# Four conditioned residual layers on one core: TensorE's register load of the language number is moved from behind layer 3's matmuls to the head of each pass

## The chip, the cores and the metric

The kernel runs on one core of a Trainium2 chip. The metric is the device time of one execution in microseconds (us). The kernel before took a median of 1185.27 us in 3 runs (1184.71 to 1189.29).

## The reference, cut to what matters

There are 128 samples, each a 128 x 512 matrix in fp32. Each sample passes through four residual layers, and each layer picks its weights by a number that belongs to the sample. The third number, the language, is the one that the change concerns.

```python
x = x + (einsum('bnh,boh->bno', x, W0[subject]) + b0[subject])          # L0
x = x + rotate_pairs(x, amplitudes ** delta_t, frequencies * delta_t)    # L1
x = x + (einsum('bsd,bdh->bsh', x, W2[category]) + b2[category])         # L2
h = relu(einsum('bsh,bha->bsa', x, W1[language]) + b1[language])         # L3
y = x + einsum('bsa,bah->bsh', h, Wup[language]) + bup[language]
x = x + layernorm(y) * gamma[language] + beta[language]
```

## The kernel before, in words

The samples are sorted by subject, so that the 1 MB matrix of layer L0 is fetched only when the subject changes (8 times). `ids` is a small SBUF tile with the sorted numbers. Each engine that needs a number reads it there into a register with `value_load`, which the trace shows as three instructions of the engine's sequencer: TENSOR_LOAD, FUSED_REGOPS and SEQ_ASSERT. Line 228 is the load of the language number (`language_of`) on whichever engine calls it, line 231 that of the "first of its subject" flag, line 222 that of the subject, line 219 that of the sample's number.

Each engine has an instruction order written out by hand, a software pipeline over the samples. Semaphores tie the engines together. TensorE (PE) does, in pass s of its loop:

- `l0_front(s + 1)`: the first 6 of L0's 12 matmuls for the next sample (lines 879 and 883). It first waits for x1 and for the rounded x, at line 877.
- `l2(s)`: L2's 12 matmuls, 4 each at lines 918, 922 and 928. The four at line 928 read `w2_lo`, the low part of the weights, which VectorE (DVE) makes in two halves at line 741. The first and the third of the four wait for one half each.
- `language_of(pe, s - 1)`: the register load.
- `l0_back(s + 1)`: the other 6 matmuls of L0 (lines 890 and 896).
- `transpose_x3(s)`: four transposes (line 938).
- `up(s - 1, lang_before)`: three matmuls with the up-projection of the sample before (lines 958, 959, 961). Their weights' address comes from the register, so this is the first place that needs the number.
- `rotate(s + 1)`: L1 as 8 short matmuls (line 907).
- `down(s)`: 8 short matmuls (line 948) on the transposed x3, which ScalarE (ACT) copies out of PSUM in four parts at line 578. Each pair of matmuls waits for its part.

The order around the loads on other engines: ACT reads the language number (line 228) once a pass, after it has copied the rotated sample (line 540), and GpSimd (POOL) reads the flag of line 231 at about the same time. SyncE (SP) issues the DMAs in this order in each step: the next L2 weights (line 289, 1 MB), the bias row (line 297, after a wait for the x3 that DVE makes at line 763), the store of a finished sample (line 312), the next x (line 281), then the flag's load (line 231), the subject's (222) and the ordinal's (234), and L3's weights (line 306). SP's steps run in a hardware loop of 12 steps a round.

Of the kernel before, what the change touches and what calls it, by code (L numbers as in the profile page):

```python
# [18 lines left out]
def conditioned_residual_stack(  # L19
# [32 lines left out]
    with ctx:  # L52
# [174 lines left out]
        def language_of(eng, s):  # L227
            return eng.value_load(ids[0:1, bass.ds(3 * B + s, 1)], min_val=0, max_val=L - 1)
# [612 lines left out]
        def _(pe):  # L841
# [26 lines left out]
            def l0_front(s):  # L868

                if s == 0:  # L870
                    pe.wait_ge(w0_hi_made[0], 1)
                    pe.wait_ge(w0_hi_made[1], 1)
                if s == 1:
                    pe.wait_ge(diag_made, 2)
                if s >= 1:
                    pe.wait_ge(x1_made, s)
                pe.wait_ge(x_hi_made, s + 1)
                for c in range(C):
                    pe.matmul(ps_l0[:, :], x_hi[s % 2][:, c * N:(c + 1) * N], w0_hi[:, c * D:(c + 1) * D],  # L879
                              start=(c == 0), stop=False)  # L880
                pe.wait_ge(x_lo_made, s + 1)
                for c in range(C // 2):
                    pe.matmul(ps_l0[:, :], x_lo[s % 2][:, c * N:(c + 1) * N], w0_hi[:, c * D:(c + 1) * D],  # L883
                              start=False, stop=False)

            def l0_back(s):


                for c in range(C // 2, C):
                    pe.matmul(ps_l0[:, :], x_lo[s % 2][:, c * N:(c + 1) * N], w0_hi[:, c * D:(c + 1) * D],  # L890
                              start=False, stop=False)
                if s == 0:
                    pe.wait_ge(b0_made, 2)
                    pe.wait_ge(w0_lo_made, 4)
                for c in range(C):
                    mm = pe.matmul(ps_l0[:, :], x_hi[s % 2][:, c * N:(c + 1) * N], w0_lo[:, c * D:(c + 1) * D],  # L896
                                   start=False, stop=(c == C - 1))
                mm.then_inc(l0_done, 1)

            def rotate(s):  # L900

                if s >= 1:
                    pe.wait_ge(x2T_lo_made, s)
                pe.wait_ge(mix_made, s + 1)
                pe.wait_ge(x1_made, s + 1)
                for c in range(C):
                    mm = pe.matmul(ps_mix[:, c * N:(c + 1) * N], x1[:, c * P:(c + 1) * P], mix[:, :],  # L907
                                   start=True, stop=True)
                mm.then_inc(mix_done, 1)

            def l2(s):

                if s >= 1:
                    pe.wait_ge(x3_made, s)
                pe.wait_ge(w2_hi_made, 2 * s + 2)
                pe.wait_ge(x2T_hi_made, s + 1)
                for c in range(C):
                    pe.matmul(ps_l2[:, :], x2T_hi[:, c * N:(c + 1) * N], w2_hi[:, c * D:(c + 1) * D],  # L918
                              start=(c == 0), stop=False)
                pe.wait_ge(x2T_lo_made, s + 1)  # L920
                for c in range(C):
                    mm = pe.matmul(ps_l2[:, :], x2T_lo[:, c * N:(c + 1) * N], w2_hi[:, c * D:(c + 1) * D],  # L922
                                   start=False, stop=False)
                mm.then_inc(l2_hi_done, 1)
                for c in range(C):
                    if c in (0, C // 2):
                        pe.wait_ge(w2_lo_made, 2 * s + 1 + c // (C // 2))
                    mm = pe.matmul(ps_l2[:, :], x2T_hi[:, c * N:(c + 1) * N], w2_lo[:, c * D:(c + 1) * D],  # L928
                                   start=False, stop=(c == C - 1))
                mm.then_inc(l2_done, 1)  # L930

            def transpose_x3(s):

                if s >= 1:
                    pe.wait_ge(x3T_made, C * s)
                pe.wait_ge(x3_made, s + 1)
                for c in range(C):
                    mm = pe.transpose(ps_x3T[:, c * N:(c + 1) * N], x3[s % X3B][:, c * P:(c + 1) * P], ident[:, :])  # L938
                mm.then_inc(x3T_done, 1)

            def down(s):

                pe.wait_ge(w1_loaded[s % 2], landed(s, 2))
                if s >= 1:
                    pe.wait_ge(h_made, s)
                for c in range(C):
                    pe.wait_ge(x3T_made, C * s + c + 1)
                    mm = pe.matmul(ps_hT[:, :], w1_in[s % 2][:, c * A:(c + 1) * A], x3T[:, c * N:(c + 1) * N],  # L948
                                   start=(c == 0), stop=(c == C - 1))
                mm.then_inc(hT_done, 1)  # L950

            def up(s, lang):

                y, here = ps_y[s % 2], bass.ds(lang * D, D)
                if s >= 2:
                    pe.wait_ge(out_made, s - 1)
                pe.wait_ge(h_hi_made, s + 1)
                pe.matmul(y[:, :], h_hi[:, :], wup_hi[:, here], start=True, stop=False)
                pe.matmul(y[:, :], h_hi[:, :], wup_lo[:, here], start=False, stop=False)
                pe.wait_ge(h_lo_made, s + 1)  # L960
                pe.matmul(y[:, :], h_lo[:, :], wup_hi[:, here], start=False, stop=True).then_inc(up_done, 1)  # L961
# [7 lines left out]
            pe.wait_ge(ids_made, 2)  # L969

            for s in range(B):
                if s < LAST:
                    l0_front(s + 1)
                l2(s)
                lang_before = language_of(pe, s - 1) if s >= 1 else None
                if s < LAST:
                    l0_back(s + 1)
                transpose_x3(s)
                if s == 1:
                    pe.wait_ge(wup_hi_made, len(wup_parts))  # L980
                    pe.wait_ge(wup_lo_made, len(wup_parts))
                if s >= 1:
                    up(s - 1, lang_before)
                if s < LAST:
                    rotate(s + 1)
                down(s)
# [51 lines left out]
```

## Time and profile before

| | |
|---|---|
| median of 3 runs | 1185.27 us |
| the profiled execution's own time | 1189.29 us |
| its span, first to last instruction | 1187.5 us |
| mean granted TensorE clock | 0.977 of full speed |
| PE busy (matmul) | 1124.6 us, 95% |
| DVE, ACT, POOL busy | 913.6, 797.2, 772.2 us |
| chain that ended last | PE 49%, SP's queue 28%, issue 13%, DMA 5% |

Durations below come from the profiled execution, whose own time lies 4.0 us above the median of the runs. An engine's name with a q (PEldq, SPq) means its sequencer: loads of registers, waits and the issue of DMAs, which don't count as busy. PEld is the weight load of a matmul, PE the matmul. Matmuls of 512 columns follow each other every 0.23 us in full flow, though the profile gives each a duration of 0.39 us, because they overlap.

### The profile page before, as it was taken

How to read it: one execution, taken by the hardware profiler on the slowest of the kernel's cores; microseconds unless marked ns; L12 is line 12 of the kernel's file. 1: busy time of each engine (PE TensorE's matmuls, PEld its weight loads, DVE VectorE, ACT ScalarE, POOL GpSimd, SP SyncE). 2: the span in 40 equal slices, each digit the busy share in tenths (PEclk: the TensorE clock that was granted, in tenths of full speed). 3: DMA queues.
4: the chain of work that ended last, by engine and by line, in shares of the span. 5: the costliest groups of instructions: out<-in, count | busy, mean ns of one | idle time of the engine just before them, and what ended most of it. 6: DMA issues, size and time to landing. Idle time of an engine off the chain costs nothing.

```text
span 1187.5 us, 29696 instructions
## 1 busy us (share of the span) xinstructions
PE 1124.6 (95%) x6040; PEld 932.9 (79%) x6040; DVE 913.6 (77%) x1345; ACT 797.2 (67%) x1828; POOL 772.2 (65%) x793
## 2 busy tenths in 40 slices
PE   5879999999999998999998999999999999999996
PEld 2768878887888877888887788878887888788884
DVE  5758788787777886777777778788787777778786
ACT  3647777777676766667766667677666766667674
POOL 6256676666666676666666666667676667666664
PEclk9889999999999999899999899999998999999998
DMA  7787886777677688767767776787688678867772
GB/s 255 266 301 234 259 271 221 241 262 268 221 257 238 225 259 262 250 219 242 249 222 264 245 256 215 245 286 244 220 254 282 215 248 251 270 217 253 243 256 78
DMA packets 96847, 289.90 MB, mean 244 GB/s; under 512 B 11406, under 2 KB 12046, under 8 KB 78828
## 3 DMA queue, kind: packets, MB, share of 16 engines
q1 hardware_dynamic: 95756, 287.22, 73.9%
q14 instruction: 175, 1.43, 0.4%
q8 instruction: 52, 0.85, 0.3%
q10 hardware_dynamic: 864, 0.40, 0.1%
HBM read 253.74 MB, written 33.84 MB: 242 GB/s over the span
## 4 chain that ended last, share of the span: by engine, by line
PE 49%; SPq 28%; issue 13%; DMA 5%; DVE 2%; POOL 1%; ACT 1%; ACTq 0%; DVEq 0%; POOLq 0%
SPq L219 6%; PE ps_hT L948 6%; PE ps_l L879 6%; PE ps_l L928 5%; PE ps_mix L907 5%; PE ps_l L918 5%; PE ps_l L922 5%; PE ps_l L896 5%; SPq L231 4%; PE ps_l L890 3%; PE ps_l L883 3%; DMA b_in<-b 3%; PE ps_x3T L938 2%; SPq L222 2%; SPq L234 2%
## 5 line engine op out<-in xcount | busy, mean ns | idle before, releaser
L741 DVE TENSOR_TENSOR w_lo<-w_in,w_hi 128x1024 fp32r<-128x1024 f32 x256 | 310.4, 1254 | 0.0
L446 POOL TENSOR_TENSOR x<-x,beta_sb 128x512 f32<-128x512 f32 x128 | 173.5, 1355 | 159.7 <-DVE ps_y L776 143.7
L533 ACT ACTIVATE w_hi<-w_in 128x1024 fp32r<-128x1024 f32 x256 | 255.3, 1045 | 8.5 <-PE ps_l L922 8.4
L578 ACT ACTIVATE x3T<-ps_x3T,minus_bup 128x128 f32<-128x128 f32 x512 | 146.5, 368 | 87.9 <-PE ps_x3T L938 87.8
L416 POOL TENSOR_TENSOR w_in<-w_in,ident 128x512 f32<-128x512 f32 x128 | 165.1, 1290 | 50.4 <-DMA w_in<-W 49.8
L756 DVE TENSOR_TENSOR x2T_lo<-ps_mix,x2T_hi 128x512 fp32r<-128x512 f32 x128 | 88.5, 691 | 116.1 <-ACT x2T_hi L540 116.1
L422 POOL TENSOR_TENSOR x_lo<-x_in,x_hi 128x512 fp32r<-128x512 f32 x128 | 166.1, 1298 | 7.0 <-ACT x_hi L505 4.7
L879 PE MATMUL ps_l<-w_hi,x_hi 128*128 128x512 f32 x512 | 156.2, 428 | 2.2 <-issue 2.2
L433 POOL TENSOR_TENSOR rstd<-var_eps,minus_half 128x1 f32<-128x1 f32 x128 | 141.4, 1104 | 18.9 <-POOL var_eps L428 0.2
L948 PE MATMUL ps_hT<-x3T,w_in 128*128 128x128 f32 x1024 | 141.5, 283 | 11.5 <-ACT x3T L578 11.5
L907 PEld LDWEIGHTS ps_mix<-mix,x 128*128 128x128 f32 x1024 | 125.5, 193 | 34.0 <-issue 34.0
L907 PE MATMUL ps_mix<-mix,x 128*128 128x128 f32 x1024 | 143.0, 283 | 5.2 <-DVE x L749 5.1
L428 POOL TENSOR_SCALAR var_eps<-square_sum 128x1 f32<-128x1 f32 x128 | 55.4, 433 | 141.7 <-ACT squares L565 140.6
L928 PE MATMUL ps_l<-w_lo,x2T_hi 128*128 128x512 f32 x512 | 139.3, 392 | 2.3 <-DVE w_lo L741 2.2
L948 PEld LDWEIGHTS ps_hT<-x3T,w_in 128*128 128x128 f32 x1024 | 129.8, 199 | 13.1 <-issue 13.1
L918 PE MATMUL ps_l<-w_hi,x2T_hi 128*128 128x512 f32 x512 | 139.6, 395 | 0.0
L896 PE MATMUL ps_l<-w_lo,x_hi 128*128 128x512 f32 x512 | 138.7, 393 | 0.0
L922 PE MATMUL ps_l<-w_hi,x2T_lo 128*128 128x512 f32 x512 | 136.9, 389 | 0.0
L763 DVE TENSOR_TENSOR x<-ps_l,b_in 128x512 f32<-128x512 f32 x128 | 88.5, 692 | 56.3 <-PE ps_l L928 56.3
L498 ACT ACTIVATE ps_diag<-ident,cos 128x128 f32<-128x128 f32 x128 | 47.6, 372 | 121.9 <-DVE mix L718 121.8
L776 DVE SCALAR_TENSOR_TENSOR ps_y<-ps_y,x 128x512 f32<-128x512 f32 x128 | 89.5, 699 | 45.4 <-PE ps_y L961 45.4
L918 PEld LDWEIGHTS ps_l<-w_hi,x2T_hi 128*128 128x128 f32 x512 | 98.1, 192 | 22.0
(108 smaller groups left out, 1914.2 us busy)
## 6 DMA issues: line engine op xcount, KB each, us to landing
w_in<-W SPq DMA_DIRECT2D x128, 1024.0 KB, 5.9
x_in<-xT SPq DMA_DIRECT2D x128, 256.0 KB, 4.5
w_in<-W SPq DMA_DIRECT2D x128, 256.0 KB, 2.6
b_in<-bias_rows SPq DMA_DIRECT2D x128, 256.0 KB, 5.5
out<-yb SPq DMA_DIRECT2D x128, 256.0 KB, 5.0
w_in<-W0T SPq DMA_DIRECT2D x8, 1024.0 KB, 4.8
wup_sb<-Wup SPq DMA_DIRECT2D x1, 2560.0 KB, 9.5
gamma_sb<-gamma SPq DMA_DIRECT2D x1, 2560.0 KB, 9.3
```

Source lines behind the costliest of these rows:

```text
L416: pool.tensor_tensor(diagonal_of(w2_in[s % WB]), diagonal_of(w2_in[s % WB]), ident[:, :].unsqueeze(1).broadcast_to([P, C, P]), ALU.add).th ...
L422: pool.tensor_tensor(x_lo[s % 2][:, :], x_in[s % XB][:, :], x_hi[s % 2][:, :].bitcast(fp32), ALU.subtract).then_inc(x_lo_made, 1)
L446: pool.tensor_tensor(x3[s % X3B][:, :], x3[s % X3B][:, :], beta_sb[:, bass.ds(lang * D, D)], ALU.add)\
L533: act.activation(w2_hi[:, halves[n]], w2_in[s % WB][:, halves[n]], ACT.Copy).then_inc(w2_hi_made, 1)
L741: dve.tensor_tensor(w2_lo[:, half], w2_in[s % WB][:, half], w2_hi[:, half].bitcast(fp32), ALU.subtract).then_inc(w2_lo_made, 1)
L879: pe.matmul(ps_l0[:, :], x_hi[s % 2][:, c * N:(c + 1) * N], w0_hi[:, c * D:(c + 1) * D], start=(c == 0), stop=False)
L896: mm = pe.matmul(ps_l0[:, :], x_hi[s % 2][:, c * N:(c + 1) * N], w0_lo[:, c * D:(c + 1) * D], start=False, stop=(c == C - 1))
L907: mm = pe.matmul(ps_mix[:, c * N:(c + 1) * N], x1[:, c * P:(c + 1) * P], mix[:, :], start=True, stop=True)
L918: pe.matmul(ps_l2[:, :], x2T_hi[:, c * N:(c + 1) * N], w2_hi[:, c * D:(c + 1) * D], start=(c == 0), stop=False)
L922: mm = pe.matmul(ps_l2[:, :], x2T_lo[:, c * N:(c + 1) * N], w2_hi[:, c * D:(c + 1) * D], start=False, stop=False)
L928: mm = pe.matmul(ps_l2[:, :], x2T_hi[:, c * N:(c + 1) * N], w2_lo[:, c * D:(c + 1) * D], start=False, stop=(c == C - 1))
L948: mm = pe.matmul(ps_hT[:, :], w1_in[s % 2][:, c * A:(c + 1) * A], x3T[:, c * N:(c + 1) * N], start=(c == 0), stop=(c == C - 1))
```

## The change: the load of the language number comes first in the pass

In pass s, TensorE now reads the language number of sample s - 1 ahead of `l0_front(s + 1)`, which is right behind `down(s - 1)` of the pass before, and no longer between `l2(s)` and `l0_back(s + 1)`. The number of instructions is the same, and so is the register's use in `up(s - 1)`. The last load, for `up(LAST)` behind the loop, stays.

```diff
             for s in range(B):
+                lang_before = language_of(pe, s - 1) if s >= 1 else None
                 if s < LAST:
                     l0_front(s + 1)
                 l2(s)
-                lang_before = language_of(pe, s - 1) if s >= 1 else None
                 if s < LAST:
                     l0_back(s + 1)
                 transpose_x3(s)
```

## Rows read from the trace of the kernel before

**Rows 1.** Busy us in 668:728: PE, PEld, DVE, ACT, POOL; clock, DMA share, GB/s.
```profile
668.00:728.00 60.00, 60.00 (x340) 51.16 (x339) 47.14 (x72) 42.59 (x100) 41.41 (x43) 1.00 0.72 231
```
**Rows 2.** Waits over the whole span: total us, times, longest.
```profile
PEld ps_l L890 <- issue: 13.3, 39, 0.6
...
PE ps_hT L948 <- ACT x3T L578: 11.5, 7, 1.8
...
SPq L297 <- DVE x L763: 9.7, 13, 1.6
```
**Rows 3.** Timeline, one pass (start us, us, what, number of instructions).
```profile
497.40 2.35 DVE L741 TENSOR_TENSOR w_lo<-w_in,w_hi 128x1024 fp32r<-128x1024 f32 x2
...
500.83 0.62 PE L890 MATMUL ps_l<-w_hi,x_lo 128*128 128x512 f32 x2
...
502.99 1.14 ACT L578 ACTIVATE x3T<-ps_x3T,minus_bup 128x128 f32<-128x128 f32 x4 [0.64 <-PE ps_x3T L938]
...
503.27 0.97 PEld L907 LDWEIGHTS ps_mix<-mix,x 128*128 128x128 f32 x8 [0.21 <-issue]
503.33 1.09 PE L907 MATMUL ps_mix<-mix,x 128*128 128x128 f32 x8
...
505.08 1.17 PE L879 MATMUL ps_l<-w_hi,x_hi 128*128 128x512 f32 x4
```
**Rows 4.** Line 228 from 499 to 510: duration ns min/median/max, first and last start.
```profile
L228 PEldq TENSOR_LOAD <-ids x2: 297/299/301, 499.8 to 508.2; - x2
...
L228 PEldq SEQ_ASSERT  x2: 18/18/18, 500.4 to 508.8; - x2
```
**Rows 5.** Line 877, the wait ahead of l0_front, from 503.9 to 505.6.
```profile
L877 PEldq EVENT_SEMAPHORE  x1: 51/51/51, 504.2 to 504.2; - x1
```
**Rows 6.** The last load (line 228, from 1175.5) and ACT's copies before it.
```profile
L228 PEldq TENSOR_LOAD <-ids x1: 303/303/303, 1176.5 to 1176.5; - x1
...
1175.34 1.15 ACT L578 ACTIVATE x3T<-ps_x3T,minus_bup 128x128 f32<-128x128 f32 x4 [3.71 <-PE ps_x3T L938]
```
**Rows 7.** Register loads over the whole span, by line and engine.
```profile
L228 PEldq TENSOR_LOAD <-ids x128: 295/307/1051, 46.6 to 1176.5; - x128
...
L231 SPq TENSOR_LOAD <-ids x127: 263/512/1063, 34.7 to 1147.2; - x127
```
**Rows 8.** The chain from 510 to 519, and the load of that pass (line 228).
```profile
516.95 0.91 PE ps_l L928 x4
517.85 0.10 issue
517.96 0.72 PE ps_l L890 x2
...
L228 PEldq TENSOR_LOAD <-ids x1: 942/942/942, 516.7 to 516.7; - x1
```
**Rows 9.** ACT's load of line 228 in 95:156, 487:506, 668:721 and 924:935.
```profile
L228 ACTq TENSOR_LOAD <-ids x7: 506/967/1112, 97.2 to 147.8; - x7
...
L228 ACTq TENSOR_LOAD <-ids x3: 592/928/1072, 487.7 to 504.5; - x3
...
L228 ACTq TENSOR_LOAD <-ids x7: 583/749/1110, 668.6 to 719.2; - x7
...
L228 ACTq TENSOR_LOAD <-ids x2: 714/718/721, 925.2 to 933.7; - x2
```
**Rows 10.** SP's issue of the store, timeline from 494 to 505.
```profile
503.18 0.36 SPq L312 DMA_DIRECT2D out<-yb  x1
```
**Rows 11.** Two single loads of PE with the store issued before each.
```profile
953.42 0.36 SPq L312 DMA_DIRECT2D out<-yb  x1
...
L228 PEldq TENSOR_LOAD <-ids x1: 944/944/944, 954.3 to 954.3; - x1
...
887.98 0.36 SPq L312 DMA_DIRECT2D out<-yb  x1
...
L228 PEldq TENSOR_LOAD <-ids x1: 298/298/298, 888.8 to 888.8; - x1
```

## The prediction

> **What bounds the kernel now.** I read the page first: PE is busy for 1124.6 us of 1187.5, and no other engine passes 914. The table of busy time by stretch then shows that in the middle of the kernel PE has no hole at all, 60.00 us of 60.00, at full granted clock [rows 1]. So any delay of a matmul there is a delay of the end. The page's chain says that this isn't so everywhere: 49% of it lies on PE, but 28% on SP's sequencer, which feeds the DMAs; in SP's stretches some us of PE are free. The list of waits comes next. The weight load of line 890, the first instruction behind the old place of the register load, was held up 39 times, 13.3 us together, by nothing but issue [rows 2]. That is the register load's present price, seen at the weight load.
>
> The timeline of one pass with the register loads beside it gives the mechanism. DVE ends the second half of w_lo at 497.40 + 2.35 = 499.75 [rows 3], and PE's load starts at 499.8 [rows 4]. The last load of the kernel shows the same at the other place: ACT's copies end at 1175.34 + 1.15 = 1176.49, and the load starts at 1176.5, while `down`'s matmuls, which the copies feed, are still running [rows 6]. So the sequencer hands matmuls on ahead of time, but a register load starts only when the last semaphore wait ahead of it is met, here 0.05 us later. What is ahead of it in the queue then covers it, or doesn't.
>
> A rule of the Trainium skill bears on this. "TensorE: Matmul & The Clock Gate", in its table and its section on the array, gives TensorE a queue of 64 instructions. By it alone one would expect the load to run far ahead of the matmuls at either place and to cost nothing. The trace agrees only in part: a few matmuls are queued, but the start is tied to the semaphore [rows 3, 4].
>
> **The change part by part.** The edit moves one load per pass, 127 in all. Nothing is added, and no DMA or semaphore moves.
>
> *Taken away at the old place.* The weight load normally runs one matmul (0.23 us) ahead of its matmul, and 0.06 us is the least (503.27 to 503.33 [rows 3]), so each of the 39 gaps hides some 0.17 us: 13.3 - 39 x 0.17 = 6.7 us reach the matmuls. The pass at 517 checks it: the load took 0.942, and the chain has 0.10 of issue and 0.72 for two matmuls that otherwise take 0.45, so 0.37 us were lost [rows 8]. Part of the 6.7 lies in stretches that SP sets. With 49% of the chain on PE I take 3.5 us as the gain, with bounds 0 and 6.7.
>
> *Cost at the new place, ordinary load.* The last wait ahead is now the fourth part of ACT's copy in `down(s - 1)`. It ends at 502.99 + 1.14 = 504.13 [rows 3]; the wait of line 877 fires at 504.2 behind it [rows 5]; the load would start at 504.18. The matmul of line 879 starts at 505.08, so there are 0.90 us of room. Needed are the load, 0.29 from its end to the end of SEQ_ASSERT (500.1 to 500.4 [rows 4]), 0.05 for the next step, 0.05 for the wait of line 877 [rows 5], 0.03 for the step behind it, and 0.06 from weight load to matmul: t + 0.48. The limit is t = 0.42 us. The median load takes 0.307 [rows 7], so the ordinary pass loses nothing and has 0.11 us to spare. At the old place the same sum is 500.83 - 499.80 = 1.03 of room for t + 0.29 + 0.05 + 0.06, so the limit was 0.63. The new place is tighter by 0.2 us. Its cover is the eight short matmuls of `down`; if it is lost, each 0.1 us costs 12.7 us.
>
> *Cost at the new place, slow load.* Loads take up to 1.05 us on PE and 1.06 on SP [rows 7]. What decides is the time since SP issued the store of a finished sample (line 312). SP's load of line 231 comes 1.7 us behind that store in every step, and its median is 0.512, twice its minimum [rows 7]. PE's load begun 0.85 us behind a store took 0.944 [rows 11]. So the store opens a slow period, which begins about 0.8 us after it and is over about 2 us after it.
>
> Where does the new load fall? In the passes in which SP has caught up with PE, it waits for x3 (line 763) before the bias row [rows 2] and stores at a fixed place in PE's pass: at 503.18 [rows 10], 1.0 us before the new load's 504.18. The nearest witness is ACT's load of line 228, 0.33 us later than the new one. In these passes it is slow every time: 7 with a median of 0.967, 3 with 0.928, 7 with 0.749, 2 with 0.718 [rows 9]. The old place of PE's load was free of this in those passes. If the slow period is already running at 504.18, the new load ends together with ACT's, so it takes t(ACT) + 0.33, and PE loses t(ACT) + 0.33 - 0.42, and 0.06 more for the second matmul (at the old place the sum gives 0.942 - 0.63 = 0.31, and 0.37 were measured [rows 8]): t(ACT) - 0.03. Sum: 7 x 0.94 + 3 x 0.90 + 7 x 0.72 + 2 x 0.69 = 15.7 us over 19 passes. All lie in stretches where SP waits for PE, so they count in full. If the period hasn't begun, they cost nothing: the bounds are 0 and 15.7. The two single loads at this distance, 0.83 to 0.87 us behind the store, went one each way (0.944 and 0.298 [rows 11]); but in the 19 passes ACT's load was never spared, and most of the new loads fall nearer 1.1 us behind the store. I take four fifths, 12.6 us.
>
> *Passes where a subject changes.* ACT's copies come late there and hold PE's `down` 7 times, 11.5 us [rows 2]. The load then starts late too, with only a pair or two of matmuls as cover, and some 0.5 us come on top each time, unless DVE or POOL are later still. Bounds 0 and 3.5; I take 1.
>
> Sum: -3.5 + 12.6 + 1 = +10.1 us. Against the profiled execution's own 1189.3 that is 1199.4; that execution lies 4.0 above the median of the runs, so the forecast is 1185.3 + 10.1 = 1195.4, taken as 1195.5.
>
> **The rivals.** Half a percent is 5.9 us, about what a measurement of this kernel can tell from no change.
>
> *Hidden after all (no change).* The slow period begins between 1.1 and 1.3 us behind the store, so the new load is back before it. For it speaks the fast load at 0.87 us [rows 11]; against it the slow one at 0.85. The sum is then -3.5 + 0 + 1 = -2.5: 1182.8, with bounds 1179 and 1189.
>
> *The gain alone (faster).* The place behind the matmuls of L2 was the one that met slow loads: in the stretch around 517 the load took 0.942 and cost 0.37 [rows 8]. If the new load misses every slow period and the queue ahead of it is enough even where subjects change, all 6.7 us return: 1178.6. It decides for this side if fewer than 2 passes stall and over 5.9 us of the gain is on the path; much of it lies in stretches set by SP, which speaks against. The queue of 64 in the Trainium skill's "TensorE: Matmul & The Clock Gate" would lead to this side too.
>
> *The ordinary load isn't covered (much slower).* If the sequencer needs 0.1 to 0.2 us more than my 0.48, for instance because the wait of line 877 costs more behind a load, every pass loses 0 to 0.1 us: up to 12.7 us on top, 1208, and to 1215 if slower passes also keep SP caught up with PE for longer, so that more passes stall. The last load of the kernel, 0.303 long, speaks for short loads there [rows 6]. "DMA: Bandwidth & Descriptors", under latency and other measured facts in the Trainium skill, gives a register load a floor of about 600 ns; by it an estimate would add (0.60 - 0.42) x 127 = 23 us. The trace disagrees, with a median of 0.307 [rows 7].
>
> **How the numbers follow.** The forecast's case, stalls in the caught-up passes, has 0.60; hidden after all 0.24; the gain alone 0.07; the ordinary load not covered 0.09. With all 19 passes and 3.5 where subjects change the first case reaches 1185.3 + 15.7 = 1201 and, if the gain isn't on the path, 1204.5; with half of the passes it gives 1190.7. Alone its range is 1190 to 1205. The range of 8 in 10 takes in the hidden case's middle: 1182 to 1206. Faster by over 0.5%: 0.07. Slower by over 0.5%: 0.60 without a low end of 0.06, and 0.09, so 0.63. Within: 0.24 and 0.06, 0.30.
>
> **What would show it.** PE's loads of line 228 start 0.05 us behind the end of ACT's copies; right. The issue waits at line 890 vanish, and new ones stand at line 879, few and long, up to 1 us. They fall into the passes behind a subject change in which SP waits for x3, and there PE's load lasts as long as ACT's plus 0.3 us. A median load of PE far from 0.30 us, small gaps at line 879 in every pass, or fast loads 1.0 us behind the store would prove steps wrong. If SP stands elsewhere in PE's pass, since its own steps slow down or it needs longer to catch up, the number of stalled passes is another one, and the sum with it.

## The result and the profile after

| kernel | runs | median us (lowest to highest) | ratio to the kernel before, 95% interval | span us | clock |
|---|---|---|---|---|---|
| before | 20 | 1184.78 (1180.97 to 1189.29) | 1 | 1187.5 | 0.977 |
| changed | 20 | 1191.71 (1184.87 to 1198.49) | 1.0057 [1.0044, 1.0070] | 1195.5 | 0.971 |

The change costs 6.9 us by the medians. The profiled execution, whose own time is 1197.32, has a span 8.0 us longer. A later series of the same kernel (E5 below) gave 1.0038 [1.0019, 1.0057]; it is slower in both, by about half a percent.

First the page's chain of the changed kernel. PE has 41% of it where it had 49%, and SP's queue 34% where it had 28%.

```profile
PE 41%; SPq 34%; issue 15%; DMA 5%; DVE 2%; POOL 1%; ACT 1%; ACTq 0%; DVEq 0%; POOLq 0%
```

The waits of the changed kernel over the whole span (total us, times, longest) answer to [rows 2]. The issue wait at line 890 is gone. Line 879, the first instruction behind the new place, has one 24 times. ACT still holds `down` 7 times.

```profile
PE ps_hT L948 <- ACT x3T L578: 10.9, 7, 1.8
PEld ps_l L879 <- issue: 10.7, 24, 1.7
...
PE ps_l L879 <- issue: 5.8, 14, 1.4
```

An ordinary pass of the changed kernel, timeline and then the rows of line 228 (ns min/median/max, first and last start), answers to [rows 3, 4].

```profile
560.53 1.14 ACT L578 ACTIVATE x3T<-ps_x3T,minus_bup 128x128 f32<-128x128 f32 x4 [0.63 <-PE ps_x3T L938]
...
561.80 1.06 PE L948 MATMUL ps_hT<-x3T,w_in 128*128 128x128 f32 x8
...
562.62 0.71 PE L879 MATMUL ps_l<-w_hi,x_hi 128*128 128x512 f32 x2
```
```profile
L228 PEldq TENSOR_LOAD <-ids x1: 299/299/299, 561.7 to 561.7; - x1
L228 PEldq FUSED_REGOPS  x1: 151/151/151, 562.1 to 562.1; - x1
L228 PEldq SEQ_ASSERT  x1: 18/18/18, 562.3 to 562.3; - x1
```

ACT's copies end at 560.53 + 1.14 = 561.67, the load starts at 561.7, and line 879's matmul comes at 562.62, 0.95 us behind the copies. That is what it was before (504.13 to 505.08 [rows 3]). The ordinary load is free.

A stalled pass of the changed kernel: the timeline, the load's rows, and the chain from 103.90 on.

```profile
105.22 1.14 ACT L578 ACTIVATE x3T<-ps_x3T,minus_bup 128x128 f32<-128x128 f32 x4 [0.77 <-PE ps_x3T L938]
...
105.34 0.36 SPq L312 DMA_DIRECT2D out<-yb  x1
...
107.96 1.16 PE L879 MATMUL ps_l<-w_hi,x_hi 128*128 128x512 f32 x4 [0.41 <-issue]
```
```profile
L228 PEldq TENSOR_LOAD <-ids x1: 1100/1100/1100, 106.4 to 106.4; - x1
L228 ACTq TENSOR_LOAD <-ids x1: 777/777/777, 106.8 to 106.8; - x1
```
```profile
106.66 0.89 PE ps_hT L948 x8
107.55 0.41 issue
107.96 1.16 PE ps_l L879 x4
```

The load starts 1.07 us behind the store and takes 1.10 us. Line 879 comes 1.60 us behind the copies' end at 106.36, so 0.65 us are lost. The chain shows 0.41 of it as issue. The rest is in the longer spacing of the last matmuls of `down`, which the profile charges to them. The sum of the prediction, t + 0.48 - 0.90, gives 0.68 here. ACT's load began 0.37 us later and was 0.32 shorter: the two ended together.

The load of line 228 in the changed kernel's caught-up stretches, PE and then ACT in each (around 97 to 152, 493 to 512, 673 to 727, 807 to 835 and 933 to 944), answers to [rows 9].

```profile
L228 PEldq TENSOR_LOAD <-ids x7: 537/932/1134, 97.3 to 150.9; - x7
L228 ACTq TENSOR_LOAD <-ids x7: 280/574/875, 97.7 to 151.3; - x7
...
L228 PEldq TENSOR_LOAD <-ids x3: 601/713/1078, 493.3 to 511.0; - x3
L228 ACTq TENSOR_LOAD <-ids x3: 290/551/721, 493.6 to 511.4; - x3
...
L228 PEldq TENSOR_LOAD <-ids x7: 376/683/907, 673.9 to 726.4; - x7
L228 ACTq TENSOR_LOAD <-ids x7: 304/447/557, 674.3 to 726.8; - x7
...
L228 PEldq TENSOR_LOAD <-ids x4: 731/853/1047, 807.2 to 833.9; - x4
...
L228 PEldq TENSOR_LOAD <-ids x2: 720/748/777, 933.4 to 942.1; - x2
```

Such rows time the passes as well. From the first to the seventh of ACT's loads six passes took 50.6 us before (97.2 to 147.8 [rows 9]) and take 53.6 now (97.7 to 151.3); in the third stretch 50.6 became 52.5, in the second, two passes, 16.8 became 17.7 (17.73 before rounding). The stretch around 807 is new: in the trace of before SP stored at another place of the pass (in the first four 0.2 to 0.4 us behind ACT's last copy, and not 1.0 ahead of it), and none of ACT's loads in it was slow.

**Where the time went.** For this table I took the end of ACT's last copy (line 578) in each pass from the traces and summed the differences by kind of stretch. "Caught up": SP waits for PE in them in the changed kernel; passes, counted from 1, 5 to 13, 15 to 17, 50 to 53, 70 to 77, 85 to 89 and 99 to 101. "SP late": the long stretches between two changes of subject (17 to 28, 30 to 41, 53 to 65, 77 to 83, 89 to 97, 101 to 111, 113 to 126). The rest are the start and the passes around a change of subject. An undisturbed pass takes 8.43 us.

```
us                          before   changed    E3      E4     undisturbed
26 passes caught up         219.3    228.8    219.3   219.3    219.3
71 passes, SP late          606.3    599.0    601.8   601.8    598.8
28 passes, the rest         293.0    299.1    296.7   306.7
pass 1 to pass 126         1118.6   1126.9   1117.8  1127.7
```

The changed kernel loses 9.5 us where SP has caught up. It gains 7.4 where SP is late, down to the undisturbed length. Of these, 5.9 are at line 890: from the last matmul of line 928 to the first of line 890, and from that to the second, the starts now stand as close as elsewhere. It loses 6.1 in the rest. The sum is 8.3.

The spacing of PE's matmuls, summed in the same way, tells what the rest is made of: 1.5 us more ahead of line 879, behind the load; 1.3 in the six matmuls of `l0_front`, where the clock is low in two more passes than before; 3.4 at line 928, where PE waits for `w_lo`; and 1.4 less at line 890.

### The profile page after: what moved, and what is told of

Its sections match the earlier page's. It is cut to its first block, busy times and chain, and to the rows that moved or that the text cites. A ratio compares the mean times of both kernels' runs of the same rounds, so it can differ in the third digit from the quotient of the medians.

```text
span 1195.5 us, 29696 instructions
## 1 busy us (share of the span) xinstructions
PE 1127.0 (94%) x6040; PEld 941.5 (79%) x6040; DVE 916.2 (77%) x1345; ACT 799.7 (67%) x1828; POOL 771.7 (65%) x793
## 4 chain that ended last, share of the span: by engine, by line
PE 41%; SPq 34%; issue 15%; DMA 5%; DVE 2%; POOL 1%; ACT 1%; ACTq 0%; DVEq 0%; POOLq 0%
SPq L219 7%; PE ps_l L879 5%; PE ps_hT L948 5%; SPq L231 5%; PE ps_l L918 4%; PE ps_l L928 4%; PE ps_l L922 4%; PE ps_mix L907 4%; PE ps_l L896 4%; SPq L222 3%; SPq L234 3%; DMA b_in<-b 3%; SPq L225 2%; SPq L228 2%; PE ps_l L883 2%
## 5 line engine op out<-in xcount | busy, mean ns | idle before, releaser
L433 POOL TENSOR_TENSOR rstd<-var_eps,minus_half 128x1 f32<-128x1 f32 x128 | 147.5, 1153 | 18.9 <-POOL var_eps L428 0.2
L907 PEld LDWEIGHTS ps_mix<-mix,x 128*128 128x128 f32 x1024 | 126.6, 194 | 34.3 <-issue 34.3
L428 POOL TENSOR_SCALAR var_eps<-square_sum 128x1 f32<-128x1 f32 x128 | 46.8, 366 | 138.2 <-ACT squares L565 137.0
L928 PEld LDWEIGHTS ps_l<-w_lo,x2T_hi 128*128 128x128 f32 x512 | 95.0, 188 | 28.6 <-DVE w_lo L741 9.7
```

## The experiments

Each ratio is to the kernel before, run on the same chip in the same series. Its median was 1193.10 us beside E1 to E4, 1191.81 beside E5 to E8, and 1193.26 beside E9 and E10.

| | kernel | median us | ratio, 95% interval | span us |
|---|---|---|---|---|
| E1 | changed, store last in SP's step | 1164.64 | 0.9774 [0.9749, 0.9799] | 1162.3 |
| E2 | before, store last | 1160.33 | 0.9731 [0.9707, 0.9756] | 1158.5 |
| E3 | load behind l0_front | 1191.24 | 0.9988 [0.9973, 1.0003] | 1186.3 |
| E4 | one load ahead of the loop | 1194.75 | 1.0020 [1.0004, 1.0037] | 1197.0 |
| E5 | changed, again | 1195.86 | 1.0038 [1.0019, 1.0057] | 1197.3 |
| E6 | load behind l0_front, store last | 1156.97 | 0.9703 [0.9680, 0.9726] | 1156.6 |
| E7 | changed, two loads a pass | 1265.43 | 1.0630 [1.0596, 1.0664] | 1261.8 |
| E8 | before, two loads a pass | 1216.41 | 1.0209 [1.0180, 1.0239] | 1211.2 |
| E9 | before, SP reads ahead of its store | 1173.50 | 0.9848 [0.9829, 0.9868] | 1168.4 |
| E10 | changed, SP reads ahead of its store | 1174.59 | 0.9856 [0.9837, 0.9874] | 1171.8 |

### E1 and E2: what opens the slow period

SP's store goes to the end of its step, behind the issue of L3's weights; E1 has PE's load at the new place, E2 at the old.

```diff
                     load_b2(s + 2, k + 2, j + 2)
-                if k >= 2:
-                    store_out(s - 2, j - 2)
                 if k < LAST - 3:
                     load_x(s + 4, k + 4, j + 4)
                     load_w0(s + 4)
                 if k < LAST - 1:
                     load_w1(s + 2, k + 2, j + 2)
+                if k >= 2:
+                    store_out(s - 2, j - 2)
```

> The changed kernel with one thing more: SP issues the store of the finished sample (store_out) as the last DMA of its step, behind L3's weights, and no longer between the bias row and the next x. Theory A (the store opens the slow period for register loads, 0.8 to 2.2 us behind its issue): where SP has caught up with PE the store now comes about 4 us behind PE's load, so PE's loads there take about 0.30 us and the issue waits at line 879 outside the passes where a subject changes vanish; the time falls by 6 to 10 us from the changed kernel, to 1182 to 1186 us. The slow loads turn up 0.8 to 2.2 us behind the store's new place, on whichever engine loads there. Theory B (the fetch of x, line 281, or the stream of L2's weights makes loads slow, not the store): x is now issued where the store was, so PE's loads in the caught-up passes stay slow (0.6 to 1.1 us) and the time stays at 1190 to 1193.

> The kernel before with the store last in SP's step, the control for the run above. Theory A: slow loads move to 0.8 to 2.2 us behind the store's new place here too. PE's load at its old place is hit in other passes than before; its limit is 0.63 us. 1180 to 1188 us, about the same as the kernel before. If the reorder alone were worth several us whatever the load's place, both store-last kernels would gain the same over their own kernels; by theory A the changed kernel gains 6 us or more from it and the kernel before 0 to 4.

The stalls went as the store's theory has it: at line 879 issue waits fell from 24 to 10, and in each caught-up stretch the mean pass is at most 8.46 us. The place of the slow loads settles it. I sorted every register load of all engines (some 1930) by the time since the last issue of a store. Seven slow loads of each run come ahead of the first store and are left out, and so are two of the kernel before at 2.5 to 2.7 us and one of 0.405 us in E1 at 3.5:

```
register loads over 0.4 us, of all, by us behind the store's issue
             0-0.5   0.5-1    1-1.5    1.5-2    2-2.5
before        0      11/38    58/74   114/158   14/140
E1            0      18/73    34/46     6/147     0
E2            0      34/87    29/35     6/129     0
```

The slow loads moved with the store, not with x's, the weights' or the bias row's issue, which now stand elsewhere to it. But the times missed the expectations by far. E1 is 28.5 us and E2 32.8 us below the kernel before of their series, and neither theory had that. Slow loads fell from 206 to 66 and 76. SP's own row shows it (line 231; before 263/512/1063 [rows 7]):

```profile
L231 SPq TENSOR_LOAD <-ids x127: 262/269/290, 34.3 to 1114.4; - x127
```

That is E2. Its chain has 70% on PE and 13% on SP's queue. E9 takes this up.

With the store last the new place still costs 4.3 us more than the old, and the traces say where: passes 68 to 70, 97 to 99 and 111 to 113, each a change of subject, took 21.2, 21.6 and 21.6 us in E1 against 19.4, 20.0 and 20.0 in E2. One of them, first the timeline of E1 and of E2, then their tables of busy time (start:end, length, busy PE, PEld, DVE, ACT, POOL, then clock), E1 and E2 again:

```profile
640.91 2.05 PE L879 MATMUL ps_l<-w_hi,x_hi 128*128 128x512 f32 x4 [0.30 <-issue]
642.75 1.05 PE L883 MATMUL ps_l<-w_hi,x_lo 128*128 128x512 f32 x2
```
```profile
640.98 1.17 PE L948 MATMUL ps_hT<-x3T,w_in 128*128 128x128 f32 x8 [1.76 <-ACT x3T L578]
641.91 1.17 PE L879 MATMUL ps_l<-w_hi,x_hi 128*128 128x512 f32 x4
```
```profile
637.00:640.00 3.00, 1.24 (x12) 1.08 (x11) 2.65 (x4) 3.00 (x8) 3.00 (x2) 1.00 0.71 214
640.91:642.75 1.84, 1.84 (x4) 1.46 (x5) 1.84 (x3) 1.74 (x6) 0.54 (x1) 0.50 0.91 362
```
```profile
638.00:641.00 3.00, 1.22 (x10) 1.02 (x9) 2.54 (x4) 2.94 (x6) 3.00 (x3) 1.00 0.82 226
641.91:643.75 1.84, 1.84 (x10) 1.53 (x10) 1.84 (x3) 1.51 (x6) 0.00 (x0) 1.00 0.97 400
```

In both kernels PE was busy for 1.2 of the 3 us shown first, since `down` waited for ACT's late copies (1.76 us in E2). In E2 PE runs on into line 879 at the granted clock 1.00. In E1 the load, an ordinary one of 0.305 us, leaves a hole of 0.30, and the clock is 0.50, the lower of the two levels (1.2 in place of 2.4 GHz); the four matmuls of line 879 take 2.05 us in place of 1.17. The hole costs 0.3 us, the clock some 1.3.

The hole alone doesn't bring the clock down. E1 has seven such passes, each with a wait of 1.76 us and then a hole of 0.26 to 0.36; the clock fell in three of them, the ones named above, and stayed at 1.00 in the other four. One of these:

```profile
297.28 1.16 PE L879 MATMUL ps_l<-w_hi,x_hi 128*128 128x512 f32 x4 [0.36 <-issue]
```

In E2, with no hole, it stayed at 1.00 in all seven. Nor is the hole needed: in the kernel before the clock was down to 0.50 before line 879, with no hole there, behind four of its six waits of 1.76 us, and in E6 behind one of seven. What else decides isn't shown.

### E3 and E4: is it the cover, and where does the gain go?

E3 puts the load behind `l0_front(s + 1)`, so that the same semaphore starts it but six matmuls of 512 columns stand ahead of it as well. E4 reads once ahead of the loop. It leaves out the other 127 loads, and so most of its up-projections are those of another language; it was meant as a floor for the time.

```diff
             for s in range(B):
-                lang_before = language_of(pe, s - 1) if s >= 1 else None
                 if s < LAST:
                     l0_front(s + 1)
+                lang_before = language_of(pe, s - 1) if s >= 1 else None
                 l2(s)
```
```diff
+            lang_before = language_of(pe, 0)
             for s in range(B):
-                lang_before = language_of(pe, s - 1) if s >= 1 else None
                 if s < LAST:
                     l0_front(s + 1)
```

> The register load stands between l0_front(s + 1) and l2(s). Theory A (a load starts when the last wait ahead of it is met, and what is queued ahead covers it): the last wait ahead is still the fourth part of ACT's copy, or the wait of line 877 behind it, so the load starts within 0.15 us of the same moment as in the changed kernel, but eight short matmuls and six long ones (0.90 + 1.37 us) are ahead. The limit rises to about 1.7 us, above the longest load seen (1.1). Loads in the caught-up passes are as slow as in the changed kernel, and none of them costs anything: no issue waits at line 918, time 1181 to 1184 us. Rival (PE's queue holds only some eight instructions ahead of a register load, or the load waits for the matmuls ahead): the load starts later, behind part of l0_front, and stalls of 0.3 to 0.6 us appear at line 918 in every pass: 1200 us or more.

> PE reads the language number once, ahead of its loop, and uses that of the first sample in every up() of the loop but the last: the other 127 register loads are left out, and so the up-projections of most samples are those of another language. It is the floor for every place of the load. Theory A: as fast as the load between l0_front and l2, 1181 to 1184 us, since SP's pace and the subject changes then set what the loads don't; the 6.7 us that reach the matmuls in the kernel before come back only in part. Rival (all of PE's load time in the trace counts): 1184.8 - 7.7 = 1177 us or less.

E3 still meets slow loads, and they cost nothing. In its first caught-up stretch (line 228):

```profile
L228 PEldq TENSOR_LOAD <-ids x7: 297/835/1144, 95.3 to 145.9; - x7
```

Seven loads with a median of 0.835 us, and the stretch runs at 8.43 a pass. No issue wait is left at lines 890 or 918. Cover is what decides at the new place. Yet E3 is no faster than the kernel before (0.9988, within its interval of 1), and E4, with no load in the loop at all, is not either (1.0020). I had expected 1 to 4 us of gain for both: E3 has 1.9 by the medians, within its interval of nothing, and E4 is 1.7 us slower. Both have the caught-up stretches undisturbed and gain 4.5 us where SP is late, and give 3.7 and 13.7 back in the rest. E3's chain has 38% on SP's queue and 34% on PE. Here SP's own load is the longer one:

```profile
L231 SPq TENSOR_LOAD <-ids x127: 265/644/1134, 33.3 to 1147.1; - x127
```

Summed over its 127 loads line 231 took 68.0 us on SP before, 70.8 in the changed kernel, 76.7 in E3 and 79.6 in E4. So what PE gains in these kernels SP does not pass on. Part of it is lost at line 928, where PE waits for `w_lo`. The waits over the whole span (total us, times, longest) in the kernel before, the changed one, E3 and E4:

```profile
PE ps_l L928 <- DVE w_lo L741: 2.2, 6, 0.7
PE ps_l L928 <- DVE w_lo L741: 4.7, 8, 1.5
PE ps_l L928 <- DVE w_lo L741: 6.5, 10, 1.4
PE ps_l L928 <- DVE w_lo L741: 5.5, 10, 1.4
```

In E3 and E4 this line accounts for most of the 3.0 us over the undisturbed length where SP is late. E4 loses 6.4 us more than the kernel before at line 961, which waits for POOL's `h_lo`. Why that is worst in the kernel with the fewest loads wasn't traced.

### E5: the changed kernel once more

No edit.

> The changed kernel itself, beside the kernel before on the same chip. On the chip of the first four runs the kernel before stood at 1193 us and not at 1185, and with one load in all PE gained nothing over it; so this tells whether the change costs the same there. Theory A (slow loads stall the passes in which SP has caught up with PE; the gain at line 890 is given back at the subject changes): 5 to 11 us over the kernel before. Rival (the difference depends on how far SP is behind, and is swallowed where SP sets the pace more): 0 to 3 us.

The intervals of the two series overlap. The medians differ by 4.1 us, which lies between the 5 to 11 of theory A and the 0 to 3 of its rival. The profile of this execution loses 6.3 us in the caught-up stretches (225.6 against 219.3). Of the 3.2 less than before, 1.7 are in the stretch around 807, which isn't disturbed here: whether SP has caught up there changes from one execution to the next.

### E6: cover and a store out of the way

E3's place with E1's order of SP.

> The load between l0_front and l2, and the store last in SP's step: the two edits that the runs so far point to. With the store last PE sets most of the time, so the 13 waits at line 890 that the kernel before with the store last still has (5.1 us at the weight load, some 3 us at the matmuls) should come back in full: 1157 to 1159 us, 1 to 3 us under that kernel (1160.3). No issue wait at line 890 and none at 879 beyond the first passes. Rival (the load there costs something where a subject changes): the same 1160 or more.

This is the fastest kernel of the study: 0.9703 [0.9680, 0.9726] of the kernel before, 35 us less, and as fast as expected. No issue wait is left at line 890, and at 879 only the two that the kernel before has too. Its median is 3.4 us below that of E2, which was taken in another series; at the change of subject in passes 97 to 99 it took 19.7 us, where E1 took 21.6.

### E7 and E8: the room, measured with a second load

```diff
                 lang_before = language_of(pe, s - 1) if s >= 1 else None
+                if s >= 1:
+                    language_of(pe, s)
```

> The changed kernel with a second register load of PE behind the first in every pass, at the new place; its value isn't used. By the sum of the prediction there are 0.90 us of room for t + 0.48; two loads take 0.30 + 0.29 + 0.02 + 0.30, so every ordinary pass lacks 0.48 and loses 0.50 to 0.55 us: a pass of 8.44 us becomes 8.94 to 9.0 us. Over 127 passes that is 64 to 70 us where PE sets the pace, less where SP does: plus 35 to 65 us on the changed kernel. Rival (loads run ahead of the matmuls in a deep queue): ordinary passes stay at 8.44 us and the time rises by under 5 us.

> The kernel before with a second register load behind the first, at the old place. The room is 1.03 us for t + 0.40; two loads make it t = 0.91, so an ordinary pass lacks 0.28 and loses 0.28 to 0.35 us: 8.72 to 8.79 us a pass, 0.2 less than at the new place. Plus 10 to 40 us on the kernel before, since SP's pace hides more of it. Rival (what counts is the number of loads and not the room): the same pass length as with two loads at the new place.

E7, the timeline of an ordinary pass (of ACT's four copies the last two), both loads of the next pass, and PE's issue waits at line 879 over the whole span:

```profile
229.82 0.63 ACT L578 ACTIVATE x3T<-ps_x3T,minus_bup 128x128 f32<-128x128 f32 x2
...
231.89 1.17 PE L879 MATMUL ps_l<-w_hi,x_hi 128*128 128x512 f32 x4 [0.25 <-issue]
```
```profile
L228 PEldq TENSOR_LOAD <-ids x2: 301/306/310, 239.4 to 240.1; - x2
...
PE ps_l L879 <- issue: 75.8, 127, 1.8
```

Line 879 comes 231.89 - 230.45 = 1.44 us behind the copies, 0.49 more than with one load. By the prediction's sum one more load takes 0.64 (start to start), and 0.30 + 0.64 + 0.48 - 0.90 = 0.52. The room at the new place was thus sized to 0.03 us. That is a pass with two ordinary loads. Slow loads come on top: 84 of PE's are over 0.4 us in E7, and the median pass takes 9.24 us and not the 8.94 to 9.0 expected. The 127 issue waits make 75.8 us, and E7's median lies 69.6 us above that of E5, 5 us over the range that I gave.

At the old place of E8 (`w_lo`, then the first matmul of line 890) the second load costs more than the sum says:

```profile
224.88 2.35 DVE L741 TENSOR_TENSOR w_lo<-w_in,w_hi 128x1024 fp32r<-128x1024 f32 x2
...
228.72 0.73 PE L890 MATMUL ps_l<-w_hi,x_lo 128*128 128x512 f32 x2 [0.25 <-issue]
```

228.72 - 227.23 = 1.49 us, where it was 500.83 - 499.75 = 1.08 [rows 3]: 0.41 more, against 0.30 + 0.64 + 0.40 - 1.03 = 0.31 by the sum. The limit of the load at the old place was nearer 0.53 than 0.63. The median pass takes 8.85 us, over the 8.72 to 8.79 expected; the time, 24.6 us above the kernel before, lies within its range, and the same second load costs far more at the new place, as the room says and the rival doesn't.

### E9 and E10: why the store's place was worth some 30 us

SP's order of DMAs is that of the kernel before, the store in the middle. Four register loads of its step are read ahead of the store. `load_w0` and `load_w1` take them as arguments.

```diff
+                if k >= 2 and k < LAST - 3:
+                    regs = is_first(sp, s + 4), subject_of(sp, s + 4), ordinal_of(sp, s + 4)
+                    lang = language_of(sp, s + 2)
                 if k >= 2:
                     store_out(s - 2, j - 2)
                 if k < LAST - 3:
                     load_x(s + 4, k + 4, j + 4)
-                    load_w0(s + 4)
+                    load_w0(s + 4, regs)
                 if k < LAST - 1:
-                    load_w1(s + 2, k + 2, j + 2)
+                    load_w1(s + 2, k + 2, j + 2, lang)
```

> The kernel before, with SP's order of DMAs as it was; only four register loads of its step (the flag, subject and ordinal of line 231, 222 and 234 and the language of line 228) are read ahead of the store of line 312 and no longer up to 3.8 us behind it. The store stays in the middle of the step. Theory: the store that was issued last in the step gained 27 to 32 us because SP's own load of line 231 no longer fell 1.7 us behind it, where it took a median of 0.51 us in place of 0.27: SP's step was 8.47 us, longer than PE's 8.43, so SP lagged through most of the kernel. Then the same gain comes here without a move of the store: L231 on SP has a median near 0.27 us, SP's mean step falls to 8.25 to 8.33, and the time is 1160 to 1170 us. Rival: it came from the DMAs' order (x and W1 no longer queued behind the store's wait or its transfer); then line 231 gets short but the time stays within 8 us of the kernel before, 1183 to 1195.

> The same four loads of SP ahead of the store, with PE's language load at the new place, at the head of the pass. If the slow period belongs to the store alone and SP waits for x3 at the bias row, the store now comes some 2.6 us later in PE's pass than in the changed kernel's caught-up passes, so behind PE's load: few loads of PE over 0.4 us, and only the passes where a subject changes cost something, as with the store last: 2 to 6 us above the kernel with the same loads ahead and the old place, 1163 to 1174 us. If the stalls of the changed kernel come from something that stays at the head of the pass whatever SP's order (the end of down, x's issue), then 10 us or more above it.

SP's load in E9:

```profile
L231 SPq TENSOR_LOAD <-ids x127: 263/270/291, 32.7 to 1122.7; - x127
```

The sum of the 127 falls from 68.0 to 34.3 us, SP's mean step (store to store, those over 11 us left out) from 8.47 to 8.25 us, and the time by 19.8 us, 1.5%. That is well off the rival's "within 8 us", and 3.5 us short of the range that I gave. So SP's own slow load, one instruction, is the likely reason why its step was longer than PE's pass of 8.43: its mean is 0.27 us shorter, and the step 0.22. E9 can't part that from what else the edit moves, since the store is issued 2.6 us later in the step and lands 2.3 us after its issue in place of 5.0. What E2 has beyond it (13 us) comes from changes of subject, above all two: passes 48 to 50 and 68 to 70 took 19.6 and 19.4 us in E2, 22.1 and 24.9 in E9. I haven't traced why.

E10 stands 1.1 us above E9 by the medians and has a ratio inside E9's interval; I had expected 2 to 6. SP waits for x3 28 times in E10, as often as in the changed kernel (27) and more often than before (13 [rows 2]). That is the condition in which the changed kernel stalled, and the stalls are nearly gone: 7 issue waits at the head of the pass, and 6 of PE's loads over 0.4 us. The timeline of E10 shows why (lines are 4 higher here):

```profile
705.16 1.14 ACT L582 ACTIVATE x3T<-ps_x3T,minus_bup 128x128 f32<-128x128 f32 x4 [0.64 <-PE ps_x3T L942]
...
707.76 0.36 SPq L312 DMA_DIRECT2D out<-yb  x1
```

The store comes 1.46 us behind the end of the copies, and not 1.0 us ahead of it.

## Why the prediction came out as it did

The forecast was 1195.5 us, 10.1 above the kernel before; measured were 6.9 by the medians and 8.0 by the spans. The stalls in the caught-up passes, which make the sign, were foreseen as they came. That the sum is so near is in part luck: by the profile the forecast's three terms, -3.5, 12.6 and 1, were -7.4, 9.5 and 6.1, and the errors offset each other. Step by step:

- **Where the load starts.** Right: 0.05 us behind the last wait ahead of it, in every pass looked at. The queue of 64 that the Trainium skill gives in "TensorE: Matmul & The Clock Gate" doesn't help a register load here: in E3 six more matmuls stand between, and its load still starts 0.2 us behind the end of ACT's copies; the matmuls cover it, since they were handed on before.
- **Ordinary load covered.** Right: line 879 is 0.95 us behind the copies as before, and E7 found the room to 0.03 us. The rival with a loss in every pass is refuted. Refuted too is, for loads away from a store, the floor of about 600 ns in "DMA: Bandwidth & Descriptors" of the Trainium skill: the median of PE's 128 loads in E2 is 0.302 us.
- **Slow load in caught-up passes.** Right in kind and place; all 19 named passes lost time. The size was off. The step was "the new load ends together with ACT's, so it takes t(ACT) + 0.33". The two mostly do end together, but ACT's load of the kernel before was no measure for the end: the 19 loads of PE took 15.05 us together, while ACT's 19 had taken 15.54, and not 0.33 more each. They ended a median of 1.86 us behind the store; ACT's had ended at 2.20. By t - 0.42 the 19 then cost 7.1 us, and 7.4 were measured, in place of 15.7, of which 12.6 were taken for the doubt whether the period had begun. (The 15.7 used the medians as if they were means; from the 15.54 it would have been 15.0.) Five more passes stalled, the new stretch around 807 and pass 16, and brought 2.1. The prediction had named that chance ("the number of stalled passes is another one") without a term for it. Together 9.5. In these records the slow period ended earlier where a load was begun earlier in it; the reason stays open.
- **Gain at the old place.** The passes where SP is late became 7.4 us shorter, 5.9 of them at line 890; over the whole kernel line 890 gives back 7.3. That is over the bound of 6.7, to which the limit of 0.53 in place of 0.63 (E8) fits. I had taken half, 3.5, since SP might swallow the rest. It is swallowed elsewhere: E4, with no load in the loop at all, is no faster than the kernel before.
- **Changes of subject.** I took +1, with bounds of 0 and 3.5, as 0.5 us for each uncovered load. The passes in which SP hasn't caught up and isn't late lost 6.1 us. Uncovered loads make 1.5 of it and the lower clock in `l0_front` 1.3, the latter in two passes, one of which has no hole; the largest piece, 3.4 us, is PE's longer waits for `w_lo` at line 928, and the forecast had no term for them. They rose in E3 and E4 as well, whose loads cost nothing. In a pass in which the clock falls behind the hole, 0.3 us become 1.6. The changed kernel shows that behind 172.57, and the kernel before at the same pass doesn't:

```profile
172.57:174.50 1.93, 1.93 (x6) 1.49 (x7) 1.93 (x4) 1.73 (x6) 0.69 (x1) 0.55 0.35 90
174.50:177.00 2.50, 2.50 (x9) 1.98 (x8) 1.96 (x3) 0.37 (x1) 2.40 (x3) 0.67 0.40 102
```
```profile
168.77:170.70 1.93, 1.93 (x10) 1.59 (x9) 1.93 (x4) 1.73 (x6) 0.69 (x1) 1.00 0.46 150
```

  Passes 13 to 15 took 1.6 us longer by it. The profile of E5, the same kernel, has the hole at this pass too, but its clock is 1.00, and passes 13 to 15 took 20.1 us as in the kernel before:

```profile
172.70 1.15 PE L879 MATMUL ps_l<-w_hi,x_hi 128*128 128x512 f32 x4 [0.26 <-issue]
```

  The last two terms together: 7.4 gained and 6.1 lost make -1.3, where the forecast had -3.5 + 1 = -2.5.

The sum of what was measured, 9.5 - 1.3 = 8.2, is close to the span's 8.0. The "hidden after all" rival needed the new load to be back before the period began; 24 issue waits, 22 more than before, say no. "The gain alone" falls with it. E10 shows what the missing stalls take: there the store comes 2.5 us later in PE's pass. Even so the new place gains nothing over the old one.

## What to carry to other kernels

A register load starts when the last semaphore wait ahead of it in its engine's queue is met, so its price is read from what is queued between that wait and its consumer: a load of 0.30 us and what follows it need 0.75 us of queued work, and more where loads are slow. Look at the spread of such loads before their number: here 180 of the 245 that began 0.8 to 2 us behind the issue of a store were slow (kernel before), and the one that seems to have mattered most stood on SP, where 0.27 us a step went with a DMA queue slower than PE. Read registers ahead of the store, or issue the store last.

## What the runs showed of the hardware that wasn't expected

- Register loads take 0.26 to 0.31 us in the main on all engines, but up to 1.24 us when begun 0.7 to 2.7 us behind the issue of a 256 KB store to DRAM (kernel before). They keep to no other DMA of the step when the order is changed. With the store last (E1, E2) the period was over earlier, by 1.5 us behind the store in nearly all cases, and the store landed 2.4 us after its issue in place of 5.0. Which of the two makes the other, or whether x's load right behind the store does both, wasn't tried; in E9 x is issued 1.2 us behind it, as in the kernel before, and the store still lands after 2.3 us, which speaks against x.
- Two slow loads on different engines often end together (107.51 and 107.55 in the stalled pass above). Of the 18 pairs of PE's and ACT's loads in the changed kernel that were both over 0.4 us, 13 ended within 0.04 us of each other, the other five 0.2 to 0.5 us apart.
- Behind a wait of 1.76 us, one short burst of matmuls and then a hole of 0.26 to 0.36 us, the granted clock was 0.50 in three of E1's seven passes and 1.00 in four. The same wait without the hole kept 1.00 in all seven of E2, but in the kernel before it went with 0.50 in four of six.
